# One-hot rows built as words of four bytes, and thirteen edge blocks kept on chip for a second pass

## The reference, cut to what matters

```python
# first network, its start (E edges)
ei = emb[atom_z[src]]; ej = emb[atom_z[dst]]
gate = silu(edge_attr @ F1W + F1b) @ F2W + F2b
gate = gate + (ei * (ej @ adapt)).sum(-1, keepdims=True)
msg = gate * h[dst] * (cw * mj)[:, None]
agg = segment_sum(msg, src)
...
# second network
seg_max = segment_max(logits, dst)
ex = exp(logits - seg_max[dst])
rst = segment_sum(soft_label[src] * (ex / segment_sum(ex, dst)[dst])[:, None], dst)
```

## Time and profile before

| what | us |
|---|---|
| median of three runs | 5577.47 (5575.12 to 5592.55) |
| the profiled execution, its own time | 5589.14 |
| its span, first to last instruction | 5587.4 |
| gate stage, blocks 1 to 24 of one-hot rows | about 1226 to 1847 |
| weigh stage | about 4060 to 4268 |

### The profile page before, as it was taken

The page is one execution under the profiler, slowest core; times in us unless marked ns, Lnnn a source line. Parts: engine busy times, 40 slices in busy tenths (PEclk is TensorE's granted clock), DMA queues, the critical chain, the costliest instruction groups (busy, mean ns, idle before and its releaser), DMA issues. The chain is left out here.

```text
span 5587.4 us, 187942 instructions
## 1 busy us (share of the span) xinstructions
PE 4125.9 (74%) x78491; PEld 3524.3 (63%) x78576; DVE 3831.4 (69%) x8933; ACT 2701.2 (48%) x8154; POOL 2683.2 (48%) x2702
## 2 busy tenths in 40 slices
PE   6888885026666489859976996799477844977886
PEld 4455553015555389849975996699456823977786
DVE  6888875149999689849966986699584446436254
ACT  3333331026666479839974996599402424100410
POOL 2777777757666267717762774377222500000000
PEclk7666665559999699969986997899697976988897
DMA  9322222248777366436634662566166342000000
GB/s 355 81 74 74 69 67 68 57 95 210 193 198 207 101 171 178 134 87 171 175 106 113 181 172 67 154 175 176 32 123 212 136 145 86 2 10 4 4 4 11
DMA packets 537236, 653.08 MB, mean 117 GB/s; under 512 B 321984, under 2 KB 369220, under 8 KB 533141
## 3 DMA queue, kind: packets, MB, share of 16 engines
q1 hardware_dynamic: 499989, 591.11, 38.0%
q0 software_dynamic: 33856, 48.44, 3.7%
q10 hardware_dynamic: 2496, 0.98, 0.1%
HBM read 460.24 MB, written 180.09 MB: 115 GB/s over the span
## 5 line engine op out<-in xcount | busy, mean ns | idle before, releaser
L299 POOL DMA_INDIRECT edges<-sb_bk_rec,sb_bk_pos x782 | 785.9, 1005 | 324.4 <-issue 234.1
L1749 ACT ACTIVATE sb_at_val<-banks,sb_at_prob 128x49 f32<-128x49 f32 x3800 | 783.0, 349 | 42.9 <-PE banks L1674 36.5
L1797 DVE CUSTOM_DVE_ANT_0 sb_at_left<-banks,sb_at_others 128x512 f32<-128x512 f32 x1000 | 644.9, 660 | 108.9 <-PE banks L1655 93.6
L1634 PE MATMUL banks<-sb_near,sb_at_hotT_d 128*128 128x49 bf16 x11100 | 617.8, 185 | 28.9 <-DVE sb_at_key L1774 10.6
L1636 PE MATMUL banks<-sb_queryp,sb_at_hotT_s 128*128 128x49 bf16 x11400 | 633.5, 186 | 5.6 <-issue 5.5
L1634 PEld LDWEIGHTS banks<-sb_near,sb_at_hotT_d 128*128 128x128 fp8e4 x11100 | 565.1, 97 | 35.9 <-issue 28.7
L1636 PEld LDWEIGHTS banks<-sb_queryp,sb_at_hotT_s 128*128 128x128 fp8e4 x11400 | 565.2, 96 | 6.7 <-issue 6.0
L1594 POOL TENSOR_TENSOR sb_at_key<-sb_at_key,sb_at_attr 128x400 f32<-128x400 f32 (+1 forms) x400 | 374.1, 936 | 371.9 <-ACT sb_at_key L1722 350.4
L1732 ACT ACTIVATE sb_at_others<-sb_at_hotT_s,sb_at_minus_big 128x1536 bf16<-128x1536 fp8e4 (+2 forms) x400 | 534.7, 1337 | 3.9 <-DVE sb_at_tops L1797 3.9
L1601 POOL TENSOR_TENSOR sb_at_val<-sb_at_val 128x490 f32<-128x490 f32 (+1 forms) x400 | 387.5, 969 | 67.3 <-ACT sb_at_val L1749 65.8
L1674 PE MATMUL banks<-sb_near,sb_at_hotT_d 128*128 128x49 bf16 x11100 | 364.6, 186 | 51.2 <-ACT sb_at_val L1749 32.2
(11 more groups left out here) (696 smaller groups left out, 10284.1 us busy)
## 6 DMA issues: line engine op xcount, KB each, us to landing
edges<-sb_pad SPq DMA_DIRECT2D x95, 460.0 KB, 7.2
sb_gt_rec<-edges SPq DMA_DIRECT2D x25, 1748.0 KB
sb_at_attr<-attr SPq DMA_DIRECT2D x100, 400.0 KB, 3.4
sb_at_attr<-attr SPq DMA_DIRECT2D x100, 360.0 KB, 4.0
sb_at_hot_s<-rows_src SPq DMA_DIRECT2D x100, 320.0 KB, 3.7
sb_we_hotT<-rows_dst_t SPq DMA_DIRECT2D x52, 592.0 KB, 5.8
sb_at_hotT_s<-rows_src_t SPq DMA_DIRECT2D x96, 320.0 KB, 3.3
sb_at_hotT_d<-rows_dst_t SPq DMA_DIRECT2D x96, 320.0 KB, 3.2
```

Of the source, the lines that this page charges most:

```text
L299: pool.indirect_dma_start(list1, bass.IndirectOffsetOnAxis(pos[:, t:t + 1], 0), rec[:, k, j, :], None).then_inc(sent[k], 16)
L1634: pe.matmul(ps[:, 0, H1 * j:H1 * j + H1], where, what, start=(n == 0), stop=(n == 2))
L1749: ins = act.mul(val[:, v % VB, j, 0, :], ps[:, 5, H1 * j:H1 * j + H1], prob[:, i % 2, k:k + 1])
L1797: dve.tensor_tensor_reduce(left[:, x % 2, 0:n], ps[:, 3 + x % 2, 0:n], others[:, w % 2, ks[0] - first:ks[-1] + 1 - first, :].rearrange("p ...
```

## The change

In the gate stage a one-hot piece is made by two instructions instead of one. Four bytes of fp8 are taken as one word of 32 bits. `at_nodes` now writes the positions as integers and derives two things with four further instructions of 76 elements (both sides at once): `quarter`, the position divided by four, as bf16, and `word`, the number whose value is 0x38 (1.0 in fp8) shifted to the right one of four bytes. `same_quarter` compares `quarter` with 0 to 31 in bf16 (32 results for an edge instead of 128), and `one_hots` multiplies the result by `word` and writes it as a 32-bit integer, which is the four bytes. In the weigh stage the ring has R = 13 buffers. The second pass begins with the last 13 blocks, which are still in them, and loads only the other 13. `sparts` is cleared only where nothing is written, `prob` not at all, and the first two blocks of logits are split ahead of the rest.

```diff
@@ -1235,7 +1235,11 @@
     near = m.sb("gt_near", [P, NW, 3, GT], BF16)
     far = m.sb("gt_far", [P, 4, 3, GT], BF16)
     rec = m.sb("gt_rec", [P, HB, KT, REC])
-    ls, ld = m.sb("gt_ls", [P, 2, KT]), m.sb("gt_ld", [P, 2, KT])
+    W4 = P // 4
+    loc, byte = m.sb("gt_loc", [P, 2, KT], I32), m.sb("gt_byte", [P, 2, KT], I32)
+    quarter, word = m.sb("gt_quarter", [P, 2, 2, KT], BF16), m.sb("gt_word", [P, 2, 2, KT], I32)
+    count = m.sb("gt_count", [P, W4], BF16)
+    same = m.sb("gt_same", [P, 2, 12, W4], BF16)
     hot_s, hot_d = m.sb("gt_hot_s", [P, HB, KT, P], F8), m.sb("gt_hot_d", [P, HB, NW, P], F8)
     hotT_s, hotT_d = m.sb("gt_hotT_s", [P, 2, KT, P], F8), m.sb("gt_hotT_d", [P, 2, NW, P], F8)
...
@@ -1422,20 +1426,36 @@
                 dve.wait_ge(s_rec[i % HB], 16 * (i // HB + 1))
                 if i >= 2:
                     dve.wait_ge(s_hot, NM * (i - 1))
-                dve.tensor_scalar(ls[:, at, :], rec[:, i % HB, :, R_SRC], -float(P * i), None, ALU.add).then_inc(s_at, 1)
-                dve.tensor_tensor(ld[:, at, :], rec[:, i % HB, :, R_DST], starts, ALU.subtract).then_inc(s_at, 1)
+                dve.tensor_scalar(loc[:, 0, :], rec[:, i % HB, :, R_SRC], -float(P * i), None, ALU.add).then_inc(s_at, 1)
+                dve.tensor_tensor(loc[:, 1, :], rec[:, i % HB, :, R_DST], starts, ALU.subtract).then_inc(s_at, 1)
                 dve.tensor_scalar(dead[:, i, :], rec[:, i % HB, :, R_SRC], 0.0, -BIG, ALU.is_lt, ALU.mult).then_inc(s_at, 1)
                 dve.wait_ge(s_at, 4 * i + 3)
                 dve.tensor_tensor(w1[:, i, :], rec[:, i % HB, :, R_W1], dead[:, i, :], ALU.add).then_inc(s_at, 1)
-
-            def one_hot(i, n):
-                side, a, b = MAKE[n]
-                if n == 0 and i >= HB:
-                    dve.wait_ge(s_outh[i % HB], 32 * (i // HB))
-                    dve.wait_ge(s_sum, Q * (i - HB + 1))
-                to, loc = (hot_s, ls) if side == "s" else (hot_d, ld)
-                dve.tensor_tensor(to[:, i % HB, a:b, :], along(c["iota"][:], b - a), bc(loc[:, i % 2, a:b], P), ALU.is_equal,
-                                  saturate=False).then_inc(s_hot, 1)
+                link(dve.tensor_scalar(byte[:], loc[:], 3, None, ALU.bitwise_and))
+                link(dve.tensor_scalar(word[:, at], byte[:], float(2 ** 26), float(531 * 2 ** 21), ALU.mult, ALU.add))
+                link(dve.tensor_scalar(loc[:], loc[:], 2, None, ALU.arith_shift_right))
+                link(dve.tensor_copy(quarter[:, at], loc[:]))
+
+            def same_quarter(i, ns):
+                for n in ns:
+                    side, a, b = MAKE[n]
+                    m, v = NM * i + n, "sd".index(side)
+                    if m >= 2:
+                        dve.wait_ge(s_hot, m - 1)
+                    dve.tensor_tensor(same[:, m % 2, 0:b - a, :], along(count[:], b - a),
+                                      bc(quarter[:, i % 2, v, a:b], W4), ALU.is_equal).then_inc(s_same, 1)
+
+            def one_hots(i, ns):
+                for n in ns:
+                    side, a, b = MAKE[n]
+                    m, v = NM * i + n, "sd".index(side)
+                    if n == 0 and i >= HB:
+                        dve.wait_ge(s_outh[i % HB], 32 * (i // HB))
+                        dve.wait_ge(s_sum, Q * (i - HB + 1))
+                    dve.wait_ge(s_same, m + 1)
+                    to = (hot_s if side == "s" else hot_d)[:, i % HB, a:b, :].bitcast(I32)
+                    dve.tensor_tensor(to, same[:, m % 2, 0:b - a, :], bc(word[:, i % 2, v, a:b].bitcast(F32), W4), ALU.mult
+                                      ).then_inc(s_hot, 1)
 
             def message(u):
                 i, q = divmod(u, Q)
@@ -1466,10 +1486,12 @@
             link(dve.tensor_copy(wbase[:, 0:KT], starts))
             link(dve.memset(acc[:], 0.0))
             link(dve.memset(gate[:], 1.0))
+            link(dve.tensor_copy(count[:], c["iota"][:, 0:W4]))
             at_nodes(0)
             dve.wait_ge(s_at, 4)
-            for n in range(NM):
-                one_hot(0, n)
+            for n in range(0, NM, 2):
+                same_quarter(0, range(n, n + 2))
+                one_hots(0, range(n, n + 2))
             for u in range(U + 4):
                 i, q = divmod(u, Q)
                 if u < U:
@@ -1477,8 +1499,8 @@
                         if q == 0:
                             at_nodes(i + 1)
                             dve.wait_ge(s_at, 4 * (i + 2))
-                        for n in MAKE_AT[q]:
-                            one_hot(i + 1, n)
+                        same_quarter(i + 1, MAKE_AT[q])
+                        one_hots(i + 1, MAKE_AT[q])
                     message(u)
                 if u >= Q + 3 and (u - 3) % Q == 0:
                     add((u - 3) // Q - 1)
@@ -2057,7 +2079,12 @@
     RG = [range(k, min(k + 8, NW)) for k in range(0, NW, 8)]
     NR = len(RG)
     J = NB + 1
-    hotT = m.sb("we_hotT", [P, 4, NW, P], F8)
+    R = 13
+    ORDER = list(range(J - R, J)) + list(range(J - R))
+    SLOT = [j % R for j in ORDER[:R]] + [j % R for j in ORDER[:J - R]]
+    LOADS = [(J - 1 - n) // R + 1 for n in range(R)]
+    EARLY = 2
+    hotT = m.sb("we_hotT", [P, R, NW, P], F8)
...
         @block.sync
         def _(sp):
-            for x in range(2 * J):
-                j = x % J
-                if x >= 4:
-
-                    if x - 4 < J:
-                        sp.wait_ge(s_laid, NR * (x - 3))
-                    else:
-                        sp.wait_ge(s_got, x - 4 - J + 1)
-                sp.dma_start(hotT[:, x % 4].rearrange("p k e -> p (k e)"), lists["hotT_d"][j]).then_inc(s_in[x % 4], 16)
+            def load(j, n):
+                sp.dma_start(hotT[:, n].rearrange("p k e -> p (k e)"), lists["hotT_d"][j]).then_inc(s_in[n], 16)
+            for j in range(J):
+                if j >= R:
+                    sp.wait_ge(s_laid, NR * (j - R + 1))
+                load(j, j % R)
+            for y in range(R, J):
+                sp.wait_ge(s_got, y - R + 1)
+                load(ORDER[y], SLOT[y])
...
@@ -2094,14 +2121,14 @@
 
         @block.tensor
         def _(pe):
-            pe.wait_ge(s_clear, 2)
+            pe.wait_ge(s_clear, 1)
             for j in range(J):
-                pe.wait_ge(s_split, 1 if j < NB else 2)
+                pe.wait_ge(s_split, 1 if j < EARLY else 3)
                 if j:
                     pe.wait_ge(s_rows, j)
                 pe.transpose(turned_bank[0:3 * KT, :], sparts[:, j].rearrange("p n k -> p (n k)"), c["identb"][:]
                              ).then_inc(s_turned, 1)
-                pe.wait_ge(s_in[j % 4], 16 * (j // 4 + 1))
+                pe.wait_ge(s_in[j % R], 16 * (j // R + 1))
                 pe.wait_ge(s_rows, j + 1)
                 for g, ks in enumerate(RG):
                     x = NR * j + g
...
             pe.wait_ge(s_max, 1)
-            for j in range(J):
-                x = J + j
-                pe.wait_ge(s_in[x % 4], 16 * (x // 4 + 1))
-                if j >= 2:
-                    pe.wait_ge(s_shift, 2 * j - 3)
+            for y in range(J):
+                if y >= R:
+                    pe.wait_ge(s_in[SLOT[y]], 16 * (LOADS[SLOT[y]] + 1))
+                if y >= 2:
+                    pe.wait_ge(s_shift, 2 * y - 3)
                 for k in range(NW):
-                    ins = pe.matmul(ps[:, 4 + j % 2, 3 * k:3 * k + 3], hotT[:, x % 4, k, :], mparts[:, k, :], start=True,
+                    ins = pe.matmul(ps[:, 4 + y % 2, 3 * k:3 * k + 3], hotT[:, SLOT[y], k, :], mparts[:, k, :], start=True,
                                     stop=True)
                 ins.then_inc(s_got, 1)
 
...
         @block.vector
         def _(dve):
             link = Link(dve, s_link)
-            dve.memset(sparts[:], 0.0).then_inc(s_clear, 1)
-            dve.memset(prob, 0.0).then_inc(s_clear, 1)
-            dve.wait_ge(s_clear, 2)
+            dve.memset(sparts[:, :, :, NW:KT], 0.0).then_inc(s_clear, 1)
 
             def divide(weight, parts, rest):
                 link(dve.tensor_copy(parts[0], weight))
                 link(dve.tensor_tensor(rest, weight, parts[0], ALU.subtract))
                 link(dve.tensor_copy(parts[1], rest))
                 dve.tensor_tensor(parts[2], rest, parts[1], ALU.subtract).then_inc(s_split, 1)
-            divide(w1[:, :, 0:NW], [sparts[:, 0:NB, n, 0:NW] for n in range(3)], srest[:, 0:NB, :])
+            for a, b in ((0, EARLY), (EARLY, NB)):
+                divide(w1[:, a:b, 0:NW], [sparts[:, a:b, n, 0:NW] for n in range(3)], srest[:, a:b, :])
             divide(w1_2, [sparts[:, NB, n, 0:NW] for n in range(3)], srest[:, NB, :])
             for j in range(J):
                 for g, ks in enumerate(RG):
...
```

More of the change, by code:

```diff
@@ L1247, in gate_edges @@
     names = ["near", "at", "hot", "turned", "copied", "rows", "emb", "prod", "msg", "rest", "split2", "sum", "added",
-             "link", "second", "back"]
+             "link", "second", "back", "same"]
```

(2 more changed lines are left out.)

24 lines of the change are left out of this document (12 added, 12 removed).

## The result

The changed kernel takes 5554.06 us, median of 9 runs (5539.06 to 5569.69), against 5587.18 us for the kernel before (9 runs, 5575.12 to 5595.7): ratio 0.9942, 95% interval 0.9927 to 0.9956, so 33 us or 0.58% faster. The forecast was 34 us faster, counted down from 5577.5 us, the median of the first three runs; from the median of nine the same 34 us lead to 5553. The profiled execution of the changed kernel took 5539.06 us, the fastest of its nine, so its whole stages are not compared with those of before: the attention stage alone, which no edit touches, is 17.8 us shorter in it. What follows is read from periods and waits inside the stages that changed.

What follows compares the result with a forecast made beforehand. It took VectorE to bound the gate stage and the weigh stage's first pass, with DMA at 0.92 in the second. Gate -8 and weigh stage -26 us, 34 off 5577.5, gave 5543, range 5488 to 5575.

Steps and rivals of the forecast that it cites:

- The turns: Gate stage: VectorE and GpSimd alternate by whole instructions, so one of a split pair is usually held 0.40 us.
- no turns: Rival, gate stage: GpSimd doesn't hold the new bf16-reading instructions; 58 us saved there, 5493 in all; chance 0.19.
- pairs: Rival, gate stage: the comparison runs bf16 at L500's faster rate; 16 us more saved, 5527; chance 0.10.
- half rate: Rival, gate stage: the mixed-type product costs a further 1.04 ns an element; +60 us, 5603; chance 0.06.
- every small instruction is held: Rival, gate stage: all four new small instructions meet GpSimd, not one; +28 us, 5571; chance 0.12.
- I take -0.35: Gate stage: net saving in us a block, from -0.43 less a part lost to `emb`; times 24, -8 us.
- The weigh stage's start, -3.3: Weigh stage: without the two memsets the maxima start at 4066 instead of 4069.26; 0 if the load takes 7.5 us.
- First pass, -6.5: Weigh stage: 13 loads issued at once remove 6.0 us of waits and 0.5 of TensorE's slow start.
- 0 if the loads are starved by GpSimd's gathers all the same: Weigh stage, first pass: lower bound of the saving, 0 instead of 6.5 us, if gathers starve the block loads.
- Second pass, -16.5: Weigh stage: nine fewer loads at 1.83 us each save 16.5 us; the pass ends 31 us after its start.
- DMA ends last by a little: Weigh stage, second pass: loads end at 31 us, just after TensorE's 26 blocks, which need 29.6.
- the ring gives only the second pass: Rival, weigh stage: start and first pass stay as before, only the second pass gains; 5553; chance 0.03.

Runs made afterwards that it cites:

- e5: Changed kernel with one input of the gate's comparison and product in PSUM, and VectorE taking a block's sum before the step's messages; 0.9904 of the kernel before.
- e7: Changed kernel with GpSimd's two remainders of each gate step reduced to one element; 5754.49 us in one execution (kernel before: 5823.15).
- e8: Kernel before with GpSimd's two remainders of each gate step reduced to one element; 5788.37 us in one execution (unedited: 5823.15).
- e12: The changed kernel, unchanged, run again on another chip; 0.9956 of the kernel before.
- e9: Changed kernel with GpSimd's 37 gathers of the weigh stage spread over its first pass; 0.9878 of the kernel before.
- e1: Only the gate's part of the change, applied to the kernel before; 0.9962 of the kernel before.

## Why the prediction was right, step by step

- **The turns.** Right. The product of 384 elements measured 866 ns for the 0.94 forecast. It was held in each of its four steps, as written, but for less than the 0.40 us that I took: it ran 0.90 us in steps 2 and 3 and 0.83 in steps 4 and 5, for 0.55 unheld. Step 6 came as written, its comparison of 192 elements held (750 ns), its product of 160 held (718), the other two not (315 and 345). The comparison at 653 ns is a hold in one step of four, as written. Step 1 held its product (782), step 0 did not (425). Of the new small instructions one was held (L1434, 505 ns mean), three were not (200). L1307's successor, L1311, takes 0.60 to 0.92 us, 0.84 in step 5, instead of up to 2.12. The rivals *no turns*, *pairs* and *half rate* fall by these rows, *every small instruction is held* by the 200 ns. (One price among the rivals was misread: L541 costs 0.78 ns an element over the simple rate, (871 - 137) / 400 less 1.05, and not "such a further 1.04".)
- **"I take -0.35" a block, -8 us.** Measured -0.44, 10.6 us: near, but two terms behind it were mis-sized and cancel. VectorE's busy time fell by 1.67 us a block (554.66 of 600 at 25.90, to 516.13 of 590 at 25.46), not by the forecast's 0.43 and gaps. Pieces and small instructions gave 0.85 of it (13.46 to 12.61 us by their groups); 0.70 came from `gate`'s sum (L1470, 3.03 us a block for 3.73), which I had not looked at. Before, it stood at up to 0.92 us in steps 2 and 3, where 0.46 and 0.41 do:

```profile
L1450 DVE TENSOR_TENSOR sb_gt_gate<-sb_gt_rec,sb_gt_dots 128x240 f32<-128x240 f32 x94 | 44.2, 471 | 3.2
L1450 DVE TENSOR_TENSOR sb_gt_gate<-sb_gt_rec,sb_gt_dots 128x288 f32<-128x288 f32 x69 | 42.3, 614 | 2.4
```

  Against it the wait for `emb` rose by 0.78 us a block (1.17 to 1.96), where I had allowed 0.08, and the gaps between more instructions took the rest. That the term came out near is luck. e5, e7 and e8 show what holds here: the loop takes back most of what VectorE saves.
- **The weigh stage's start, -3.3.** Right: 5.9 us to the first maximum for 9.3.
- **First pass, -6.5: mis-sized.** It took 142.2 us for 144.4, -2.3. The lower bound I wrote ("0 if the loads are starved by GpSimd's gathers all the same") is what was near: the eleventh block's maximum still waited 3.19 us. The loads issued at once landed late, after up to 61.6 us, with the engines at 0.96 and only 109 GB/s while the gathers ran; more slots don't make a load land sooner.
- **Second pass, -16.5: mis-sized, and the wrong step in it is "DMA ends last by a little".** To the start of the next stage it took 39.5 us for 51.6, -12.1. The loads were done by about 4208; TensorE ended last, with 10.9 us of pauses on nothing of the program. The trace of before had 0.3 us of "issue" there, and its packets of q8 came no faster (3.9 to 8.3 us apart); TensorE waited for data at those moments anyway. A second limit, TensorE's instructions, stood right behind the first.

Weigh stage together -17.8 for -26, gate -10.6 for -8: 28 us by the traces for 34, and 33 by the medians, whose interval (25 to 41) holds both. The mechanism of the turns was right, but that 33 stands so close to 34 is in part luck: the weigh stage gave two thirds of its forecast, about what the rival *the ring gives only the second pass* has in all (16.5 us), and the rest is made up by the gate and the spread of the runs.

**Open.** Why the pauses of the first pass are some 36 us on three chips and absent on the first, with the same gathers at the same DMA share, and what VectorE and ScalarE wait for in them. Why these chips need 240 to 270 us more in all: most of it lies ahead of the gate, whose first instruction stands at 1410.2 us in e12 and at 1202.0 in the first trace. Why the gate's block is 26.20 and not 25.90 there before the change. And by what means loads under way make the instruction packets start late.

## What to carry to other kernels

A hold that an instruction suffers from a neighbour engine moves with the gaps between instructions: cutting one long instruction into two gives the neighbour a turn in between, and the price is a hold on the second. Before taking an engine's saved time as the kernel's, follow the loop that feeds it: here 3.1 us of VectorE's work was worth 0.6. Count the instructions of a fast engine as traffic: a change that removes a wait for data while DMA stays full can lay bare the wait for instructions. And look at small gathers issued in a bunch: spreading them over a stage was worth 46 us on the chip of e12, where the whole change is worth 25. On the first chip there is little to gain by it, as the pass took 142.2 us there and 137.3 in e9.

## What the runs showed of the hardware

- With one of two inputs in PSUM, VectorE's 384-element instructions took 547 to 553 ns beside GpSimd's, against 653 and 866 with both in SBUF. The hold is there with f32 inputs (0.40 us on the piece of 768 elements before) and with bf16 and int32 ones (0.28 to 0.36 us on the product of 384).
- TensorE takes its instructions in packets of 16 KB, 256 instructions, on queue q8. When block loads kept the DMA engines full, the packets started 5.8 to 7.2 us apart instead of 3.5 to 3.8, and TensorE paused 2.1 to 2.9 us after each 126 to 128 matmuls with as many weight loads. The Trainium skill ("DMA: Bandwidth & Descriptors", section "Queues, rings and completion order") has each DMA engine take its queues in turn, a packet at a time. By that an instruction packet would wait for one packet of the loads, 0.17 us as an estimate (q1 took 89.2% of 16 engines in 30 us for 2448 packets), and pauses of 2 to 3 us don't agree with it, unless what waits is longer than a packet.
- While 37 gathers of GpSimd ran one behind the other, VectorE and ScalarE stood up to 22.6 and 36.6 us beside inputs that were there, on three chips and not on the first (112 GB/s at a share of 0.95 in e12, 27 GB/s at 0.85 in e1).
